# Attention's product with v and the dense projection follow three slots behind a head's scores instead of two

## The chip, the cores and the metric

The kernel runs on one core of one Trainium2 chip. The metric is the time of one execution on the device in microseconds. Besides that there is one profiled execution of the kernel before, whose trace is read below.

## What is computed

Input x is 8 items of 512 rows by 256 columns, in float32. Three blocks follow each other: a feed-forward block, attention, and the feed-forward block once more, each on the layer-normed x and added to x. The change lies in attention alone, which is, cut to what matters:

```python
q  = (ln(x) @ w_q)                       # 16 heads of 128 columns
k, v = split(ln(x) @ w_kv)               # 4 groups of 128 columns each; 4 heads share a group
scores = q @ k.T * 128**-0.5             # 512 x 512 per item and head, causal
probs  = softmax(where(causal, scores, -inf))
ctx    = probs @ v                       # 512 x 128 per item and head
x      = x + concat(ctx) @ w_dense
```

## The kernel before

Attention works in slots, one for each item b and head h: `slot(b, h)`, 8 times 16 of them, and then a few more with no new head. Each engine has its own program and calls its own `slot` in the same order, so that the order of the code is the order of the work on each engine, and semaphores tie the engines together. n is a head's number over all items, from 0 to 127. The 512 query rows are 4 tiles, i = 3 down to 0; tile i sees (i + 1) x 128 keys, since the scores are causal.

Every product with float32 data is made of three matmuls (`product`), of a high part and a low part of each operand. So whatever feeds a product is split first: ScalarE writes the high part, VectorE the low one.

What one head goes through:

1. **Scores** (TensorE, `scores`, slot n): tiles 3, 2, then the projection of the next head's q, then tiles 1, 0. There are three banks for four tiles: tile 0 uses tile 3's bank and waits until tile 3's exponential has been taken (`e_done`).
2. **Maximum and exponential**, same slot: VectorE reduces a tile to its negative maximum (L1316), ScalarE takes the exponential (L1406).
3. **Split of the probabilities**, next slot: ScalarE L1415 and VectorE L1332, four tiles in a row at the head of the slot, to 16-bit floats in `prob`. There is one buffer `prob`: tile i may be written when the transfer of the previous head's tile i has landed (`t_landed`). L1332 reads two operands from SBUF, the exponentials and the high half.
4. **Transposing transfers**: the queue of SyncE (`dma_start_transpose`, L1171), four for each head, from `prob` to `turned`. A transfer waits for its tile (`p_lo`) and until GpSimd has emptied that tile of `turned` for the head before (`t_cast`).
5. **Casts** (GpSimd, `cast_turned`, L1470): `turned` in 16 bits to `pT` in 32, four a head. There is one `pT`, so the casts of head n wait until the product with v of head n - 1 is done:

```python
pool.wait_ge(t_landed[i], 16 * (n + 1))
reach(pool, c_ready, n)
pool.tensor_copy(cast(i), turned[:, 0:i + 1, :, i * P:(i + 1) * P]).then_inc(t_cast, 1)
```

6. **Product with v** (`attend`, at the very start of TensorE's slot n + 2): it waits for all four casts of its head.
7. **Split of ctx** (`split_context`): ScalarE L1421 after its four splits of the probabilities, VectorE L1339 after the maximum of tile 3.
8. **Dense projection** (`dense`, slot n + 2, after scores 1 and 0).

Between these lie other products at fixed places (`projections`): q of the next head in nearly every slot, after scores 2; k of the next group at the end of slots 2, 7, 11 and 15; quarters of v at the end of slots 0 and 3 to 6 and inside slots 0 and 1; the transposes of the next item's normed x in slot 14. The layer norm of the next item lies at the end of VectorE's slots 8 to 12. `add_to_x` (L1347, two instructions on VectorE) adds the dense sums of an item at the end of slot 1 of the next.

Of the kernel before, what the change touches and what calls it, by code (L numbers as in the profile page):

```python
# [955 lines left out]
K_COLS = GROUPS * D  # L956
PT_STEP = 3 * P
PT_COLS = 15 * P
PROB_SCALE = 2.0 ** 15
PROB_AT = (0, P, 3 * P, 6 * P)  # L960
PROB_COLS = 10 * P
# [80 lines left out]
def attention_slots(slot):  # L1042

    def run(eng):
        for b in range(B):
            for h in range(HEADS):
                slot(b, h)
        slot(B, 0)
        slot(B, 1)
    return run  # L1050


# [5 lines left out]
def unit(b, h, lag):  # L1058

    item, head = (b, h - lag) if h >= lag else (b - 1, h - lag + HEADS)  # L1060
    number = item * HEADS + head
    if isinstance(b, int) and not 0 <= number < B * HEADS:
        return None
    return item, head, number


def attention(nc, m, w_q, w_kv, w_dense, out):
    with ExitStack() as ctx:
# [112 lines left out]
        def _(pe):  # L1181
# [60 lines left out]
            def dense(u, half):  # L1242
                b, h, n = u
                if half == 0:
                    pe.wait_ge(c_lo, n + 1)
                if h == 0:

                    reach(pe, x_added, 2 * b - 1 + half)
                for t in (2 * half, 2 * half + 1):
                    mm = product(dn[half][:, (t % 2) * C:(t % 2 + 1) * C], lambda a: cT[:, h % 2, a, t * P:(t + 1) * P],  # L1250
                                 lambda c: wd[:, c, 0, h * C:(h + 1) * C], h == 0 and t % 2 == 0, h == HEADS - 1)
                if h == HEADS - 1:
                    mm.then_inc(d_ready, 1)

            def slot(b, h):
                now, prev2 = unit(b, h, 0), unit(b, h, 2)

                def place(p):
                    what = projections(h).get(p)
                    if what and has_projection(b, h, what):  # L1260
                        project(b + 1 if h >= 14 and what in NEXT_ITEM else b, use_index(b, h, p), what)

                if prev2:
                    attend(prev2)
                if now:
                    scores(now, 3)
                    scores(now, 2)
                place("B")
                if now:
                    scores(now, 1)  # L1270
                    scores(now, 0)
                place("C")
                if prev2:
                    dense(prev2, 0)
                place("D")
                if prev2:
                    dense(prev2, 1)
                place("E")
                place("F")

# [5 lines left out]
        def _(dve):  # L1286
# [60 lines left out]
                    dve.tensor_tensor(x, x, dn[half][:], ALU.add).then_inc(x_added, 1)  # L1347

            def slot(b, h):
                now, prev, prev2 = unit(b, h, 0), unit(b, h, 1), unit(b, h, 2)  # L1350

                def place(p):
                    what = projections(h).get(p)
                    if what and has_projection(b, h, what):
                        split(use_index(b, h, p), what)

                if prev:
                    prob_rsum(prev, 0)
                    for i in reversed(range(QT)):
                        split_probs(prev, i)  # L1360
                if now:
                    score_max(now, 3)
                if prev2:
                    split_context(prev2)
                if now:
                    score_max(now, 2)
                    score_max(now, 1)
                    score_max(now, 0)
                place("B")
                if now:  # L1370
                    prob_rsum(now, 2)
                place("C")
                place("D")
                place("E")
                if not (isinstance(b, int) and b >= B - 1):

                    if 8 <= h < 12:
                        layer_norm(b + 1, h - 8)
                    if 9 <= h < 13:
                        layer_norm_apply(b + 1, h - 9)  # L1380
                place("F")
                if h == 1 and prev2:
                    add_to_x(b - 1)

            for t in range(QT):
# [7 lines left out]
        @block.scalar  # L1393
        def _(act):
            def split(n, what):
                raw, hi, _ = use_halves(n, what)
                act.wait_ge(pj_ready, n + 1)
                act.activation(hi, raw, ACT.Copy, scale=SCALE if what[0] == "q" else 1.0).then_inc(pj_hi, 1)

            def exponential(u, i):  # L1400
                _, h, n = u
                act.wait_ge(s_max, done_of(n, i))

                reach(act, p_lo, done_of(n - 1, i))
                at, width = PROB_AT[i], (i + 1) * P
                act.activation(expo[:, at:at + width], scores_bank(i)[:, 0:width], ACT.Exp, bias=s_bias[:, h % 2, i:i + 1],  # L1406
                               accum_out=p_sum[:, h % 2, i:i + 1]).then_inc(e_done, 1)

            def split_probs(u, i):
                _, h, n = u  # L1410
                act.wait_ge(r_done, 4 * n + 4 - i // 2 * 2)

                reach(act, t_landed[i], 16 * n)
                at, width = PROB_AT[i], (i + 1) * P
                act.activation(prob_half(0, i), expo[:, at:at + width].rearrange("p (j k) -> p j k", k=P), ACT.Copy,  # L1415
                               scale=p_factor[:, h % 2, i:i + 1]).then_inc(p_hi, 1)

            def split_context(u):
                _, h, n = u
                act.wait_ge(c_ready, n + 1)  # L1420
                act.activation(cT[:, h % 2, 0], cx[:], ACT.Copy, scale=1.0 / PROB_SCALE).then_inc(c_hi, 1)  # L1421

            def slot(b, h):
                now, prev, prev2 = unit(b, h, 0), unit(b, h, 1), unit(b, h, 2)

                def place(p):
                    what = projections(h).get(p)
                    if what and has_projection(b, h, what):
                        split(use_index(b, h, p), what)

                if prev:
                    for i in reversed(range(QT)):
                        split_probs(prev, i)
                if prev2:
                    split_context(prev2)
                if now:
                    exponential(now, 3)
                    exponential(now, 2)
                place("B")
                if now:  # L1440
                    exponential(now, 1)
                place("C")
                if now:
                    exponential(now, 0)
                place("D")
                place("E")
                place("F")

            for n, what in enumerate(PROLOGUE):
                split(n, what)  # L1450
            attention_slots(slot)(act)
# [85 lines left out]
```

## Time and profile before

| | |
|---|---|
| median of 3 runs | 2898.04 us (2894.21 to 2900.98) |
| the profiled execution's own time | 2891.25 us |
| its span | 2889.5 us |
| mean granted clock of TensorE in the span | 0.975 |
| first feed-forward block | 0 to about 852 us |
| weights of attention, then its slots | to about 885 us, then 885 to 2051 us |
| second feed-forward block | 2051 us to the end |
| TensorE busy over the span | 2683.8 us (93%) |
| VectorE, ScalarE, GpSimd busy | 2175.4, 947.2, 910.9 us |

Times in the timelines are microseconds from the span's start, so that slots can be laid beside each other. Busy time counts overlapping instructions of an engine once. In brackets behind an instruction stands how long its engine had been idle before it, and who released it.

### The profile page before, as it was taken

The numbers are of one execution on the slowest core, as the hardware profiler recorded it, in microseconds if no ns is written. First come the engines' busy times: TensorE is split into PE (matmuls) and PEld (weight loads), VectorE is DVE, ScalarE is ACT, GpSimd is POOL, SyncE is SP. The second block draws the span as 40 slices with busy tenths as digits, with TensorE's granted clock in tenths as the row PEclk, the third lists the DMA queues.
The fourth block names the chain that finished last, engine by engine and source line by source line (L and its number), as shares of the span: only waits on it lengthen the run. The fifth ranks groups of instructions, "written<-read, shape, count | busy, mean of one in ns | idle before, by whom it ended". The sixth has DMA issues, their size and how long they took to land. (4 is left out here: it accounts for less than half of the span.)

```text
span 2889.5 us, 47699 instructions
## 1 busy us (share of the span) xinstructions
PE 2683.8 (93%) x15460; PEld 2424.8 (84%) x15460; DVE 2175.4 (75%) x5550; ACT 947.2 (33%) x2560; POOL 910.9 (32%) x1944
## 2 busy tenths in 40 slices
PE   6999999999967898989998989898799999999998
PEld 5999999999956787778787877777699999999997
DVE  5888888888866676667776777666678888888887
ACT  3111111111115666656665666666311111011110
POOL 4332333323212333233433333333333333323331
PEclk8999999999988999999999999999799999999999
DMA  6000000000022333333333333333400000000000
GB/s 175 1 1 1 1 1 1 1 1 1 1 72 47 74 74 74 71 74 75 75 74 74 74 74 74 75 72 74 126 19 8 1 8 9 8 1 8 9 8 8
DMA packets 386935, 117.43 MB, mean 41 GB/s; under 512 B 346752, under 2 KB 385664, under 8 KB 386688
## 3 DMA queue, kind: packets, MB, share of 16 engines
q1 hardware_dynamic: 386688, 114.39, 17.8%
q8 instruction: 124, 2.03, 0.3%
q14 instruction: 123, 1.01, 0.1%
HBM read 26.24 MB, written 4.19 MB: 11 GB/s over the span
## 5 line engine op out<-in xcount | busy, mean ns | idle before, releaser
L444 PE MATMUL ffn_ring<-ffn_mix_weights,ffn_yT 128*128 128x384 f32 x6144 | 1250.7, 345 | 16.3 <-DVE ffn_mix_weights L672 8.5
L444 PEld LDWEIGHTS ffn_ring<-ffn_mix_weights,ffn_yT 128*128 128x128 f32 x6144 | 1087.8, 191 | 61.4 <-issue 8.7
L611 DVE SCALAR_TENSOR_TENSOR ffn_mix_sums<-ffn_ring,ffn_w,ffn_mix_sums 128x384 f32<-128x384 f32 x896 | 550.9, 616 | 247.0 <-PE ffn_ring L444 228.0
L1470 POOL CAST attn_probsT<-attn_turned 128x1024 fp32r<-128x1024 f16 (+3 forms) x512 | 372.8, 735 | 726.8 <-DMA attn_turned<-attn_probs 683.8
L495 PE MATMUL ffn_ring<-ffn_out_weights,ffn_avT 128*128 128x512 f32 x1536 | 440.8, 398 | 3.1 <-POOL ffn_avT L903 3.1
L1316 DVE TENSOR_REDUCE attn_score_neg_max<-attn_scores 128x1 f32<-128x512 f32 (+3 forms) x512 | 248.5, 488 | 190.3 <-PE attn_scores L1220 181.7
L1185 PE MATMUL attn_ctx<-attn_probsT,attn_v 128*128 128x256 f32 (+2 forms) x1536 | 290.0, 340 | 97.6 <-POOL attn_probsT L1470 97.3
L1185 PEld LDWEIGHTS attn_ctx<-attn_probsT,attn_v 128*128 128x128 f32 x1536 | 251.8, 197 | 133.9 <-POOL attn_probsT L1470 114.0
L1185 PE MATMUL attn_scores<-attn_kT,attn_qT 128*128 128x256 f32 (+2 forms) x1536 | 328.5, 342 | 11.7 <-ACT attn_exponentials L1406 10.2
L1406 ACT ACTIVATE attn_exponentials<-attn_scores,attn_score_neg_max 128x512 f32<-128x512 f32 (+3 forms) x512 | 268.2, 527 | 168.9 <-DVE attn_score_neg_max L1316 165.8
L495 PEld LDWEIGHTS ffn_ring<-ffn_out_weights,ffn_avT 128*128 128x128 f32 x1536 | 283.0, 189 | 29.1 <-POOL ffn_avT L903 4.6
L1185 PEld LDWEIGHTS attn_scores<-attn_kT,attn_qT 128*128 128x128 f32 x1536 | 248.0, 194 | 31.6 <-ACT attn_exponentials L1406 12.2
L626 DVE SCALAR_TENSOR_TENSOR x<-ffn_ring,ffn_w_out,x 128x256 f32<-128x256 f32 x512 | 247.8, 484 | 17.2 <-PE ffn_ring L495 10.2
L1332 DVE SCALAR_TENSOR_TENSOR attn_probs<-attn_exponentials,attn_prob_factor,attn_probs 128x512 f16<-128x512 f32 (+3 forms) x512 | 253.7, 556 | 8.6 <-ACT attn_probs L1415 8.4
L1415 ACT ACTIVATE attn_probs<-attn_exponentials,attn_prob_factor 128x512 f16<-128x512 f32 (+3 forms) x512 | 249.8, 553 | 28.9 <-DVE attn_prob_factor L1325 25.3
L630 DVE SCALAR_TENSOR_TENSOR ffn_out_odd<-ffn_ring,ffn_w_out,ffn_out_odd 128x256 f32<-128x256 f32 x448 | 212.8, 475 | 0.0
L1185 PE MATMUL attn_projections<-attn_zT,attn_wq 128*128 128x512 f32 x768 | 211.8, 410 | 1.0 <-DVE attn_zT L1311 1.0
L1185 PE MATMUL attn_dense<-attn_wd,attn_ctxT 128*128 128x256 f32 x1536 | 209.4, 284 | 2.8 <-DVE attn_ctxT L1339 2.8
L764 ACT ACTIVATE ffn_yT<-ffn_transposes 128x256 fp32r<-128x256 f32 x64 | 24.6, 384 | 566.0 <-PE ffn_transposes L415 565.9
L1185 PEld LDWEIGHTS attn_dense<-attn_wd,attn_ctxT 128*128 128x128 f32 x1536 | 188.9, 189 | 3.8 <-DVE attn_ctxT L1339 3.2
L1185 PEld LDWEIGHTS attn_projections<-attn_zT,attn_wq 128*128 128x128 f32 x768 | 136.6, 191 | 24.7 <-DVE attn_zT L1311 1.4
L901 POOL CAST ffn_avT<-ffn_av 128x128 fp32r<-128x128 f32 x64 | 18.5, 290 | 430.8 <-DVE ffn_av L665 430.8
(134 smaller groups left out, 2740.4 us busy)
## 6 DMA issues: line engine op xcount, KB each, us to landing
attn_turned<-attn_probs SPq DMA_TRANSPOSE x512, 2.5
ffn_mix_stage<-in_L_ffn_q_proj_dram SPq DMA_DIRECT2D x32, 128.0 KB, 2.6
ffn_mix_stage<-in_L_ffn_k_proj_dram SPq DMA_DIRECT2D x32, 128.0 KB, 2.6
ffn_mix_stage<-in_L_ffn_v_proj_dram SPq DMA_DIRECT2D x32, 128.0 KB, 3.0
ffn_out_stage<-in_L_ffn_o_proj_dram SPq DMA_DIRECT2D x16, 256.0 KB, 3.4
out_dram<-x SPq DMA_DIRECT2D x8, 512.0 KB, 3.0
x<-in_L_attn_x_dram SPq DMA_DIRECT2D x7, 512.0 KB, 8.0
attn_weight_stage<-in_L_attn_w_q_dram SPq DMA_DIRECT2D x4, 512.0 KB, 8.8
```

Of the source, the lines that this page charges most:

```text
L444: last = pe.matmul(bank[:, 0:QKV], yT[:, t % 2, h, k * P:(k + 1) * P], wm[:, e, wh, k], start=(n == 0), stop=(n == 3 * CK - 1))
L495: last = pe.matmul(bank[:], avT[:, t % 2, h], wo[:, g, wh], start=(i == 0), stop=(i == 2))
L611: dve.scalar_tensor_tensor(into, bank[:, 0:QKV], w[:, t, e:e + 1], into, ALU.mult, ALU.add).then_inc(mix_done, 1)
L626: dve.scalar_tensor_tensor(x, bank[:, 0:C], wt[:, 2 * g:2 * g + 1], x, ALU.mult, ALU.add)
L630: dve.scalar_tensor_tensor(odd[:, t % 2], bank[:, C:2 * C], wt[:, 2 * g + 1:2 * g + 2], odd[:, t % 2], ALU.mult, ALU.add).then_inc(out_don ...
L764: act.activation(yT[:, t % 2, 0], tr[:, 0:C], ACT.Copy).then_inc(yT_hi, 1)
L1185: mm = pe.matmul(out_ap, stationary(a), moving(c), start=first and n == 0, stop=last and n == 2, skip_group_check=True)
L1316: dve.tensor_reduce(s_bias[:, h % 2, i:i + 1], scores_bank(i)[:, 0:(i + 1) * P], AX.X, ALU.max, negate=True).then_inc(s_max, 1)
L1332: dve.scalar_tensor_tensor(prob_half(1, i), expo[:, at:at + width].rearrange("p (j k) -> p j k", k=P), p_factor[:, h % 2, i:i + 1], prob_h ...
L1406: act.activation(expo[:, at:at + width], scores_bank(i)[:, 0:width], ACT.Exp, bias=s_bias[:, h % 2, i:i + 1], accum_out=p_sum[:, h % 2, i: ...
L1415: act.activation(prob_half(0, i), expo[:, at:at + width].rearrange("p (j k) -> p j k", k=P), ACT.Copy, scale=p_factor[:, h % 2, i:i + 1]). ...
L1470: pool.tensor_copy(cast(i), turned[:, 0:i + 1, :, i * P:(i + 1) * P]).then_inc(t_cast, 1)
```

## The change

The distance between a head's scores and its product with v and dense projection becomes a constant, `LAST_LAG = 3`, in the programs of TensorE, VectorE and ScalarE. `unit(b, h, lag)` gives the head that lies `lag` slots back. `attend`, `dense` and `split_context` now work on the head of three slots ago. The split of the probabilities stays one slot behind, and the programs of SyncE and GpSimd are as before. There is one more slot after the last head, and `add_to_x` moves from slot 1 to slot 2. No buffer is added.

```diff
+LAST_LAG = 3
@@ attention_slots
-        slot(B, 0)
-        slot(B, 1)
+        for h in range(LAST_LAG):
+            slot(B, h)
@@ TensorE
-                now, prev2 = unit(b, h, 0), unit(b, h, 2)
+                now, last = unit(b, h, 0), unit(b, h, LAST_LAG)
...
-                if prev2:
-                    attend(prev2)
+                if last:
+                    attend(last)
...
-                if prev2:
-                    dense(prev2, 0)
+                if last:
+                    dense(last, 0)
                 place("D")
-                if prev2:
-                    dense(prev2, 1)
+                if last:
+                    dense(last, 1)
@@ VectorE
-                now, prev, prev2 = unit(b, h, 0), unit(b, h, 1), unit(b, h, 2)
+                now, prev, last = unit(b, h, 0), unit(b, h, 1), unit(b, h, LAST_LAG)
...
-                if prev2:
-                    split_context(prev2)
+                if last:
+                    split_context(last)
...
-                if h == 1 and prev2:
+                if h == LAST_LAG - 1 and last:
                     add_to_x(b - 1)
@@ ScalarE
-                now, prev, prev2 = unit(b, h, 0), unit(b, h, 1), unit(b, h, 2)
+                now, prev, last = unit(b, h, 0), unit(b, h, 1), unit(b, h, LAST_LAG)
...
-                if prev2:
-                    split_context(prev2)
+                if last:
+                    split_context(last)
```

## Rows read from the trace of the kernel before

**Rows 1.** Windows, attention: length, busy (instructions) of PE, PEld, DVE, ACT, POOL; clock; DMA; GB/s

```profile
885.00:2052.00 1167.00, 1053.73 (x6508) 896.50 (x6508) 801.05 (x2017) 725.41 (x1914) 399.87 (x568) 0.98 0.36 73
```

**Rows 2.** Waits, 870 to 2075 us: engine, line, releaser; us in total, times, longest

```profile
PE attn_ctx L1185 <- POOL attn_probsT L1470: 97.3, 67, 4.0
```

**Rows 3.** One line (L1171), SyncE's transfers: ns min/median/max; issue to landing

```profile
L1171 SPq DMA_TRANSPOSE attn_turned<-attn_probs x512: 1183/1232/2698, 893.7 to 2040.7; - x171
...
DMA to landing us min/median/max: 2.3/2.5/4.8
```

**Rows 4.** Timeline, slot after a k projection: start, us, engine, line, what

```profile
1248.77 2.10 PE L1185 MATMUL attn_ctx<-attn_probsT,attn_v 128*128 128x512 f32 x12
...
1250.47 1.93 DVE L1332 SCALAR_TENSOR_TENSOR attn_probs<-attn_exponentials,attn_prob_factor,attn_probs 128x512 f16<-128x512 f32 x4
...
1252.32 0.68 DVE L1316 TENSOR_REDUCE attn_score_neg_max<-attn_scores 128x1 f32<-128x512 f32 x1
...
1253.98 0.60 PE L1185 MATMUL attn_scores<-attn_kT,attn_qT 128*128 128x256 f32 x3
...
1257.06 1.27 DVE L1332 SCALAR_TENSOR_TENSOR attn_probs<-attn_exponentials,attn_prob_factor,attn_probs 128x512 f16<-128x512 f32 x2
```

**Rows 5.** Timeline, slot that starts at 1312.83 us (item's last head)

```profile
1312.83 2.18 PE L1185 MATMUL attn_ctx<-attn_probsT,attn_v 128*128 128x512 f32 x12
...
1315.99 0.69 DVE L1316 TENSOR_REDUCE attn_score_neg_max<-attn_scores 128x1 f32<-128x512 f32 x1
...
1317.54 0.63 PE L1185 MATMUL attn_scores<-attn_kT,attn_qT 128*128 128x256 f32 x3 [0.66 <-ACT attn_exponentials L1406]
```

**Rows 6.** Timeline of PE and of POOL: a product with v and the cast it releases

```profile
1259.40 3.89 PE L1185 MATMUL attn_ctx<-attn_probsT,attn_v 128*128 128x512 f32 x12 [3.31 <-POOL attn_probsT L1470]
...
1263.42 1.04 POOL L1470 CAST attn_probsT<-attn_turned 128x1024 fp32r<-128x1024 f16 x1 [3.21 <-PE attn_ctx L1185]
```

**Rows 7.** Groups by shape (L1470): all casts of the two widest tiles

```profile
L1470 POOL CAST attn_probsT<-attn_turned 128x1024 fp32r<-128x1024 f16 x128 | 133.4, 1042 | 575.8 <-DMA attn_turned<-attn_probs 542.9 <-PE attn_ctx L1185 33.0
...
L1470 POOL CAST attn_probsT<-attn_turned 128x768 fp32r<-128x768 f16 x128 | 106.2, 829 | 15.3 <-DMA attn_turned<-attn_probs 7.0
```

**Rows 8.** Timeline: VectorE's four splits with one narrow cast, then with two casts

```profile
2012.27 2.08 DVE L1332 SCALAR_TENSOR_TENSOR attn_probs<-attn_exponentials,attn_prob_factor,attn_probs 128x512 f16<-128x512 f32 x4
2012.80 0.48 POOL L1470 CAST attn_probsT<-attn_turned 128x256 fp32r<-128x256 f16 x1 [0.69 <-DMA attn_turned<-attn_probs]
...
1929.40 2.43 DVE L1332 SCALAR_TENSOR_TENSOR attn_probs<-attn_exponentials,attn_prob_factor,attn_probs 128x512 f16<-128x512 f32 x4
1929.73 1.57 POOL L1470 CAST attn_probsT<-attn_turned 128x512 fp32r<-128x512 f16 x2 [2.16 <-DMA attn_turned<-attn_probs]
```

**Rows 9.** Timeline, slot after a quarter of v at the end of the slot before

```profile
1184.24 2.10 PE L1185 MATMUL attn_ctx<-attn_probsT,attn_v 128*128 128x512 f32 x12
...
1187.33 0.68 DVE L1316 TENSOR_REDUCE attn_score_neg_max<-attn_scores 128x1 f32<-128x512 f32 x1
```

**Rows 10.** Timeline, a slot with layer norm, to the splits of the next

```profile
1272.27 0.68 DVE L1316 TENSOR_REDUCE attn_score_neg_max<-attn_scores 128x1 f32<-128x512 f32 x1
...
1278.03 1.93 DVE L1332 SCALAR_TENSOR_TENSOR attn_probs<-attn_exponentials,attn_prob_factor,attn_probs 128x512 f16<-128x512 f32 x4
```

**Rows 11.** Group of L1347 (`add_to_x`)

```profile
L1347 DVE TENSOR_TENSOR x<-x,attn_dense 128x512 f32<-128x512 f32 x16 | 10.3, 680 | 1.1 <-PE attn_dense L1185 1.1
```

**Rows 12.** Timeline of PE: the first two products with v

```profile
900.97 3.89 PE L1185 MATMUL attn_ctx<-attn_probsT,attn_v 128*128 128x512 f32 x12 [3.18 <-POOL attn_probsT L1470]
...
912.30 1.04 PE L1185 MATMUL attn_ctx<-attn_probsT,attn_v 128*128 128x512 f32 x4
```

**Rows 13.** Timeline: the last two products with v, the last dense projection

```profile
2036.19 2.20 PE L1185 MATMUL attn_ctx<-attn_probsT,attn_v 128*128 128x512 f32 x12 [0.59 <-POOL attn_probsT L1470]
...
2043.49 3.75 PE L1185 MATMUL attn_ctx<-attn_probsT,attn_v 128*128 128x512 f32 x12 [2.04 <-POOL attn_probsT L1470]
...
2048.65 1.64 PE L1185 MATMUL attn_dense<-attn_wd,attn_ctxT 128*128 128x256 f32 x12 [1.41 <-DVE attn_ctxT L1339]
```

## The prediction, as it was made

> **What bounds the kernel now.** I read the page's busy shares first, then the windows by stage, then the waits of the attention stage, and last the timeline of single slots. Of the 1167 us of attention TensorE is busy 1053.7 us, VectorE 801 us, GpSimd 400 us [rows 1]: TensorE sets the pace, and its idle time is 113.3 us. The table of waits names almost all of it: 67 times the matmuls of `attend` stand waiting for the casts of GpSimd, 97.3 us in all [rows 2]. The casts in turn wait for transposing transfers. A transfer takes SyncE's queue 1.23 us and lands 2.5 us after its issue [rows 3], four in a row, so with the cast behind them the chain from a head's split to its `attend` is longer than many slots are. Where no such wait is met, a slot runs at TensorE's own pace. So what the change aims at is real, and bounded: those 97.3 us, and what TensorE's clock loses around the longest waits.
>
> **What it removes.** With three slots in between, the casts of a head are done a slot before its `attend`. Casts of head n are still tied to `attend` of head n - 1, which now starts slot n + 2; they end in that slot, and `attend` of n starts slot n + 3. The wait goes. Of the 97.3 us, 3.2 lie in the first slot with an `attend` [rows 12] and 0.6 + 2.0 in the last two [rows 13], costed below; the middle is 91.5 us. The lower clock: after its longest waits `attend` takes up to 3.89 us instead of 2.10 [rows 4, 6], the granted clock being at the lower of its two levels, 1.2 instead of 2.4 GHz, for a part of it. The mean of 0.98 in attention [rows 1] is 2% of 1167 us, 23 us of full speed, part of it lost while TensorE waited anyway. I take 10 us, between 0 (new waits take the old ones' place) and 20.
>
> **What it moves, the head.** The first `attend` and dense leave slot 2. Before, slot 2 lasted from 900.97 - 3.18 = 897.8 to 912.3 us, 14.5 us [rows 12]. Without those two, the wait and the low clock I count some 7.4 us of ScalarE and VectorE work from one slot's splits to the next (an estimate from 1257.06 - 1250.47 = 6.6 [rows 4], with k's split added). Gain 7.1 us. **The tail.** A third slot without scores follows. Before, from the first of them (2036.19 - 0.59 = 2035.6) to the last dense projection's end (2048.65 + 1.64 = 2050.3) it takes 14.7 us [rows 13]. Now three rounds: `attend` 2.2, 1.41 for the split of ctx, dense 1.64 make 5.3 us [rows 13]; the second and third start when the casts that waited for the `attend` before are done, 2.2 + 0.13 + 1.04 + 0.83 + 0.62 + 0.40 = 5.2 us (the durations below). So 16.2 us, 1.5 more.
>
> **What it moves, the casts.** This is the part that decides. Now the casts come at the pace of landing transfers. The transfer can't go out before the first split is made, so with 2.5 us to landing [rows 3] the first cast comes more than 1.70 + 2.5 = 4.2 us into the slot, when VectorE's splits are over (1.70 + 1.93) [rows 4]; only the narrow last ones reach the next slot's splits. After the change all four have their data long before, and start one behind the other when `attend` ends. `attend` takes 2.10 us [rows 4], and GpSimd starts 0.13 us behind its end (1263.42 - 1259.40 - 3.89) [rows 6], so 2.23 us into every slot, for 2.9 us: the casts take 1.04 and 0.83 us [rows 7], and by their slope of 0.21 us for 256 elements the two narrow ones 0.62 and 0.40. At that time VectorE is in its four splits of the probabilities: in the slot after a k projection they start 1.70 us into the slot and last 1.93 [rows 4]. The trace shows what a meeting costs: with one cast of 0.40 us between them the four splits take 2.08 instead of 1.93 us, with casts of 0.62 and 0.40 us they take 2.43, and the casts themselves stretch too (0.48, and 1.57 for the two) [rows 8]. So the two engines take turns. A cast of 0.40 costs VectorE 0.15, one of 0.62 costs 0.35, which is the cast's length less 0.26; by the same rule the casts of 1.04 and 0.83 us, which hardly meet a split now, cost 0.78 and 0.57.
>
> The Trainium skill, SBUF — State Buffer, section "Who interferes with whom", gives the mechanism a name: a VectorE instruction with two SBUF inputs contends with a GpSimd instruction that reads SBUF, and by it the second to issue is blocked until the first finishes. By that rule each meeting would cost the cast's whole length; here 1.02 us of casts cost 0.50 us, about half of it [rows 8]. What the sum would be by the full length is a rival below.
>
> How late VectorE may be: TensorE needs the bank of tile 3 for tile 0's scores 5.21 us into a slot (1253.98 - 1248.77) [rows 4]. That bank is free 1.55 us after VectorE's maximum of tile 3 starts (1317.54 - 1315.99) [rows 5]. So the maximum may start 3.66 us in; what it starts later, TensorE waits.
>
> - After k (slots 0, 3, 8, 12): the maximum starts 3.55 us in now [rows 4]. The first split runs on, three follow behind casts of 1.04, 0.83 and 0.62 us: 0.78 + 0.57 + 0.35 = 1.70, less some overlap at the first, 1.56. It starts at 5.1, a wait of 1.45 us.
> - After full layer norm (slots 10, 11): from the maximum to the next splits 5.76 us [rows 10] against 4.74 with a lighter norm [rows 4]; I take 5.3, between them, as VectorE there also meets late casts that will be gone. TensorE's next slot could begin 2.11 us after tile 0's scores (1259.40 - 3.31 - 1253.98) [rows 4, 6], so 1.55 + 2.11 = 3.66 us after the maximum if it waits. So the splits start 1.6 us in, as after k: 1.4 us.
> - After a quarter of v, and in slots 9 and 13 (seven slots: 1, 4 to 7, 9, 13): the maximum at 3.09 [rows 9], splits from about 1.2 us in, two behind casts: 0.78 + 0.57 = 1.35, less overlap 1.25. At 4.3, a wait of 0.65.
> - Slot 15 has no q projection ahead of scores 1 and 0 and waits already, 0.66 us [rows 5], so VectorE's delay counts whole: 1.3. Slots 2 and 14, with nothing extra before them: the last split alone meets a cast; 0.2 together, a guess between 0 and 1.
> - `add_to_x` is 2 x 0.68 us [rows 11], and stood ahead of slot 2's splits, under a wait. It moves ahead of slot 3's, which are late after k: 0.8 more there.
>
> An item: 4 x 1.45 + 2 x 1.4 + 7 x 0.65 + 1.3 + 0.2 + 0.8 = 15.5 us. Eight items make 124, less 8 for the first slots of the first item and for the last item's missing layer norm: 116 us. Bounds: nothing, if VectorE's splits get ahead of the casts; 186 by the full length (16 x 0.26 x 3 to 2 casts more).
>
> **The sum.** 91.5 + 10 + 7.1 - 1.5 = 107 us gained, 116 us lost: +9 on the profiled execution's 2891.25 us, 2900. That execution lies 6.8 us below the median of the runs shown, so against them 2907 us. The waits change their name and place, from `attend` to scores of tile 0.
>
> **Rivals.**
> 1. *The splits win part of the turns.* After v the third split is issued some 0.1 us to either side of the cast. If it comes first only one split is delayed, and the maximum starts at 3.7, no wait. Then only the late slots pay: 15.5 less 4.55, 1.3 and 0.2 is 9.5 an item, 48 us less: 2859 us. For it: the margin is tenths. Against it: after a quarter of v VectorE's maximum is already at 3.09 us and starts the moment the splits are over [rows 9], so they start 1.2 us in, a little behind.
> 2. *No toll worth the name*, because casts of 1.04 us yield where narrow ones did not. The whole gain stays: 2907 - 116 + 8 = 2799 us (`add_to_x` makes slot 3 late by itself: 3.55 + 1.3 is 1.2 over 3.66, seven times). This is the case on the other side together with rival 1; it decides as soon as the toll is under some 98 us. For it: no row shows a wide cast meeting a split.
> 3. *The full length.* Each meeting costs 0.26 us more: some 3 x 6 + 2 x 8 = 34 meetings an item, 8.8 us, 70 in all: 2977 us. Rows 8 speak against it.
> 4. *The transfers' loop.* Transfers now wait for casts that wait for `attend`: first cast done at 2.23 + 1.04 = 3.3, the last of four issued 3 x 1.23 later and landed 2.5 after that [rows 3], 9.5 us after the slot's start. ScalarE wants to overwrite the last tile some 2 us into the next slot, the shortest being 1259.40 - 3.31 - 1248.77 = 7.32 us long [rows 4, 6]: 9.3. Mostly even. Stragglers (longest 4.8 us to landing, 2.7 on the queue [rows 3]) used to have a us or more of slack there and lose it: a tenth of the slots (13) by 1.5 us is 20 us: 2927.
>
> **How the numbers follow.** Forecast case 0.42 (2885 to 2935); rival 1 0.25 (2830 to 2885), rival 2 0.12, rival 3 0.09, rival 4 0.12. A measurement of this kernel tells about 0.2%, 6 us, from no change. Faster: 0.25 + 0.12 + 0.05 of the forecast case = 0.42; same (2892 to 2904) 0.12; slower 0.46. The range 2825 to 2950 leaves out rival 2 and most of rival 3; since both signs hold much of the chance, the forecast case's own range stands above.
>
> **What would show it.** Right: no wait of `attend` for casts; casts released by `attend`, not by transfers; all four 2.2 to 5.5 us into the slot; VectorE's four splits at 3.2 to 3.6 us instead of 1.93 where they start late; TensorE's scores of tile 0 waiting for exponentials, some 110 us in place of 10; fewer long `attend`s. Wrong: splits still at 1.93 us would mean rival 2; ScalarE's splits waiting for transfers, rival 4; casts stretched and splits not, rival 1. What would break the sum most easily is the toll per meeting, which I take from narrow casts and apply to wide ones, 34 times an item.

## The result, and the profile after

The changed kernel takes 2917.62 us (median of 5 runs, 2911.47 to 2920.84) against 2898.04: a ratio of 1.0064, with a 95% interval of 1.0047 to 1.0081. It is some 19 us slower, or 0.6%, which is small but clear of the spread of the runs. The profiled execution took 2917.62 us, span 2915.8.

The busy times on the page of the changed kernel:

```profile
PE 2684.2 (92%) x15460; PEld 2429.6 (83%) x15460; DVE 2315.7 (79%) x5550; ACT 931.4 (32%) x2560; POOL 938.4 (32%) x1944
```

The windows of its attention stage (columns as in [rows 1]), and its waits there (columns as in [rows 2]):

```profile
885.00:2080.00 1195.00, 1058.22 (x6508) 904.17 (x6508) 940.60 (x2013) 709.59 (x1914) 427.25 (x568) 0.98 0.33 71
```

```profile
POOL attn_probsT L1471 <- PE attn_ctx L1186: 747.6, 127, 9.2
...
PE attn_scores L1186 <- ACT attn_exponentials L1407: 128.3, 113, 2.6
...
ACT attn_probs L1416 <- DMA attn_turned<-attn_probs: 10.3, 15, 1.4
```

The wait of [rows 2], 97.3 us of `attend` for casts, is gone. In its place TensorE waits 113 times for an exponential, 128.3 us in all, and 112 of these waits stand ahead of tile 0's scores. In the kernel before there were 15 of them (same window as [rows 2]):

```profile
PE attn_scores L1185 <- ACT attn_exponentials L1406: 10.2, 15, 1.2
```

VectorE grew from 801 to 940.6 us with the same instructions [rows 1]. The groups of the two pages say where, before and then after (names, count, then busy us and mean ns, then idle time ahead of them):

```profile
L1332 DVE SCALAR_TENSOR_TENSOR attn_probs<-attn_exponentials,attn_prob_factor,attn_probs 128x512 f16<-128x512 f32 (+3 forms) x512 | 253.7, 556 | 8.6 <-ACT attn_probs L1415 8.4
```

```profile
L1333 DVE SCALAR_TENSOR_TENSOR attn_probs<-attn_exponentials,attn_prob_factor,attn_probs 128x512 f16<-128x512 f32 (+3 forms) x512 | 407.4, 854 | 14.4 <-ACT attn_probs L1416 14.2
```

Those are the splits of the probabilities: the same 512 instructions, 556 ns each before and 854 ns now. One slot shows how they got there. This is the timeline of the slot after a k projection, the same head as in [rows 4] (start, length in us, engine, line, what):

```profile
1250.42 2.10 PE L1186 MATMUL attn_ctx<-attn_probsT,attn_v 128*128 128x512 f32 x12
...
1252.12 3.63 DVE L1333 SCALAR_TENSOR_TENSOR attn_probs<-attn_exponentials,attn_prob_factor,attn_probs 128x512 f16<-128x512 f32 x4
...
1252.65 3.36 POOL L1471 CAST attn_probsT<-attn_turned 128x1024 fp32r<-128x1024 f16 x4 [6.24 <-PE attn_ctx L1186]
...
1255.68 0.68 DVE L1317 TENSOR_REDUCE attn_score_neg_max<-attn_scores 128x1 f32<-128x512 f32 x1
...
1257.22 0.62 PE L1186 MATMUL attn_scores<-attn_kT,attn_qT 128*128 128x256 f32 x3 [1.40 <-ACT attn_exponentials L1407]
```

The casts now have their data (they waited for `attend`, not for a transfer), begin 2.23 us into the slot, in the middle of the splits, and the splits take 3.63 us instead of 1.93. The maximum starts 5.26 us into the slot instead of 3.55. TensorE waits 1.40 us for the bank.

### The profile page after: what moved, and what is told of

Its sections match the earlier page's. It is cut to its first block and busy times, and to the rows that moved or that the text cites. A ratio compares the mean times of both kernels' runs of the same rounds, so it can differ in the third digit from the quotient of the medians.

```text
span 2915.8 us, 47699 instructions
## 1 busy us (share of the span) xinstructions
PE 2684.2 (92%) x15460; PEld 2429.6 (83%) x15460; DVE 2315.7 (79%) x5550; ACT 931.4 (32%) x2560; POOL 938.4 (32%) x1944
## 3 DMA queue, kind: packets, MB, share of 16 engines
q14 instruction: 123, 1.01, 0.1%
## 5 line engine op out<-in xcount | busy, mean ns | idle before, releaser
L1471 POOL CAST attn_probsT<-attn_turned 128x1024 fp32r<-128x1024 f16 (+3 forms) x512 | 404.9, 829 | 769.9 <-PE attn_ctx L1186 747.6
L1186 PE MATMUL attn_scores<-attn_kT,attn_qT 128*128 128x256 f32 (+2 forms) x1536 | 338.3, 341 | 129.8 <-ACT attn_exponentials L1407 128.3
L1333 DVE SCALAR_TENSOR_TENSOR attn_probs<-attn_exponentials,attn_prob_factor,attn_probs 128x512 f16<-128x512 f32 (+3 forms) x512 | 407.4, 854 | 14.4 <-ACT attn_probs L1416 14.2
L1317 DVE TENSOR_REDUCE attn_score_neg_max<-attn_scores 128x1 f32<-128x512 f32 (+3 forms) x512 | 237.2, 481 | 47.0 <-PE attn_scores L1221 46.0
L1186 PE MATMUL attn_ctx<-attn_probsT,attn_v 128*128 128x256 f32 (+2 forms) x1536 | 271.2, 326 | 0.0
L1186 PEld LDWEIGHTS attn_ctx<-attn_probsT,attn_v 128*128 128x128 f32 x1536 | 243.6, 190 | 19.8
L1186 PE MATMUL attn_dense<-attn_wd,attn_ctxT 128*128 128x256 f32 x1536 | 219.7, 293 | 4.8 <-DVE attn_ctxT L1340 4.8
L1186 PE MATMUL attn_projections<-attn_zT,attn_wq 128*128 128x512 f32 x768 | 217.8, 420 | 1.0 <-DVE attn_zT L1312 1.0
L1186 PEld LDWEIGHTS attn_dense<-attn_wd,attn_ctxT 128*128 128x128 f32 x1536 | 199.6, 198 | 6.6 <-DVE attn_ctxT L1340 5.4
```

The lines of the kernel that those rows point to most:

```text
L1186: mm = pe.matmul(out_ap, stationary(a), moving(c), start=first and n == 0, stop=last and n == 2, skip_group_check=True)
L1317: dve.tensor_reduce(s_bias[:, h % 2, i:i + 1], scores_bank(i)[:, 0:(i + 1) * P], AX.X, ALU.max, negate=True).then_inc(s_max, 1)
L1333: dve.scalar_tensor_tensor(prob_half(1, i), expo[:, at:at + width].rearrange("p (j k) -> p j k", k=P), p_factor[:, h % 2, i:i + 1], prob_h ...
```

## The experiments

Each ratio is to the kernel before, timed on the same chip: its median was 2898.0 us beside e1 to e4, 2895.57 beside e5 to e8, 2890.55 beside e9 to e11. Two of the eleven, e3 and e4, have one run each.

**e1: casts only behind the next head's four splits.** In the changed kernel, on GpSimd, ahead of a head's first cast:

```
+ if i == QT - 1 and n + 1 < B * HEADS:
+     pool.wait_ge(p_lo, done_of(n + 1, 0))
```

> The changed kernel, and GpSimd's four casts of a head wait for VectorE's four splits of the next head's probabilities (one wait ahead of the first cast). Theory (casts and splits take turns at SBUF): the splits are back at 1.93 us (now 2.4 to 3.6), TensorE's waits for exponentials fall from 128 us to 10 to 25 us, and nothing takes their place, since the casts still end a slot ahead of the product with v: 2917 less some 110, plus 20 for transfers that start 1 us later and stragglers among them: 2826 us, 2800 to 2860. Rival (the loop of casts, transfers and the overwriting of the probabilities is what limits at three slots): the later casts make it worse, ScalarE's waits for transfers grow from 10 us to over 100, and the time is 2900 or more. Rival (the third slot's order costs by itself, whatever the casts do): no change, 2917.

Measured: 2893.58 us, ratio 0.9987 (0.9976 to 0.9999). Splits and casts no longer meet, but the time hardly moved. Its waits, and its group of splits:

```profile
ACT attn_probs L1416 <- DMA attn_turned<-attn_probs: 190.6, 243, 3.1
DVE attn_probs L1333 <- ACT attn_probs L1416: 151.2, 207, 3.0
...
PE attn_scores L1186 <- ACT attn_exponentials L1407: 105.5, 96, 2.9
```

```profile
L1333 DVE SCALAR_TENSOR_TENSOR attn_probs<-attn_exponentials,attn_prob_factor,attn_probs 128x512 f16<-128x512 f32 (+3 forms) x512 | 264.9, 549 | 153.5 <-ACT attn_probs L1416 151.2
```

The splits are back at 549 ns each, so the meetings were what made them long. But ScalarE now waits 190.6 us to overwrite `prob` until transfers have read it. That is the loop of the prediction's rival 4: a later cast empties `turned` later, the transfer goes out later, the split of the next head waits. In the slot whose `attend` starts at 1185.51 us ScalarE's second split stands 1.81 us for a transfer. The theory had put this loop at 20 us and missed by 68; of the expectation's first rival, the loop itself, the wait came as said (over 100 us) and the time nearly (2900 or more). So the run shows half of the point: the meetings lengthen the splits. What they cost in time it can't show, since another wait took their place.

**e2: the same wait, one split earlier** (`done_of(n + 1, 1)`: the last split may meet the first cast).

> As the run before, but the casts wait only for three of the four splits, so that the first cast (1.04 us) may meet the narrowest split. Theory: the last split is held up by some 0.7 us where it comes behind the cast, which makes the maximum of tile 3 start at about 3.6 us in early slots (no wait) and 4.3 in late ones (0.6 us of wait in six of sixteen slots): 20 to 30 us slower than the run before. If meetings of a wide cast and a split cost next to nothing, equal to it, or faster by the 0.4 us that the transfers start earlier.

Measured: 2856.0 us, 0.9854 (0.9835 to 0.9872), 37.6 us faster than e1. The waits:

```profile
ACT attn_probs L1416 <- DMA attn_turned<-attn_probs: 115.0, 139, 2.6
...
PE attn_scores L1186 <- ACT attn_exponentials L1407: 80.8, 82, 2.8
```

The theory missed again, and in its sign: with casts one narrow split earlier (0.34 us, the least of the splits' durations in e1) ScalarE waits 75.6 us less for transfers, which is worth far more than the 14 us that the splits grew (279.1 us). So a little time of the casts costs much where they sit in a closed loop, and e1's time was set by that loop.

**e3 and e4: the kernel before, with four more instructions of GpSimd on each head.** They stand where the changed kernel has its casts, behind `attend`, and write the same `pT`, which the real casts then write again. In e3 they are copies that read the weights of v; in e4 they only write zeros. (`extra` counts them, and the real casts wait for it.)

```
+ if i == QT - 1:
+     reach(pool, c_ready, n)
+     for k in reversed(range(QT)):
+         pool.tensor_copy(cast(k), <weights of v, same size>).then_inc(extra, 1)   # e3
+         pool.memset(as_f32(cast(k)), 0.0).then_inc(extra, 1)                      # e4
+     pool.wait_ge(extra, QT * (n + 1))
```

> The kernel before (two slots), and GpSimd makes four more copies a head, of the casts' sizes, from the weights of v (SBUF) into the place of the casts, as soon as the product with v has read it; the real casts follow and overwrite them. They start 2.2 us into the slot, where the changed kernel has its casts. Theory: VectorE's splits stretch to 2.4 to 3.6 us and the scores of tile 0 wait for exponentials, as in the changed kernel, with the waits of the product with v kept besides: 2970 to 3060 us. Rival (not the meetings but the change of order costs): splits at 1.93, within 30 us of the kernel before.

> As the run before, but the four extra GpSimd operations only write (memset of the same places), read nothing. If splits and casts fight over a read path alone, as the Trainium skill's page SBUF — State Buffer, section Who interferes with whom, has it for two SBUF inputs against a GpSimd instruction that reads: splits at 1.93 us, and the time within 30 us of the kernel before (GpSimd's busy time alone may delay a cast). If any GpSimd work on SBUF holds up the splits: as with the copies.

Measured: e3 2934.2 us, e4 2893.46 us, one run each. The groups of the splits, e3 and then e4:

```profile
L1332 DVE SCALAR_TENSOR_TENSOR attn_probs<-attn_exponentials,attn_prob_factor,attn_probs 128x512 f16<-128x512 f32 (+3 forms) x512 | 361.2, 766 | 6.7 <-ACT attn_probs L1415 6.7
```

```profile
L1332 DVE SCALAR_TENSOR_TENSOR attn_probs<-attn_exponentials,attn_prob_factor,attn_probs 128x512 f16<-128x512 f32 (+3 forms) x512 | 253.5, 556 | 9.5 <-ACT attn_probs L1415 9.4
```

With copies the splits grow by 108 us and TensorE waits 71.8 us for exponentials; with writes at the same place they stay at 253.5 us, to 0.2 us what they were. So it is GpSimd's reading of SBUF that holds VectorE up, not its being busy, and with no change of lag at all. The Trainium skill, SBUF — State Buffer, section "Who interferes with whom", says the same: an instruction of VectorE with two SBUF inputs contends with one of GpSimd that reads SBUF, not with one that only writes it. The two traces agree, 361.2 against 253.5 us. e3 fell short of its expected 2970. The expectation had kept the waits of `attend` for casts besides, and they fell, from 97.3 to 64.4 us: part of the new wait replaced the old one. The splits grew less than in the changed kernel, too (361.2 against 407.4 us); why, no run was made for.

**e5: two buffers `turned` in the changed kernel.** It opens the loop: a transfer waits for the casts of two heads back. To make room only the tiles below the diagonal are kept, and `pT` is laid out in 13 tiles.

```
- turned = sb("turned", [P, QT, HL, SEQ], F16)
+ turned = sb("turned", [P, 2, HL * PROB_COLS], F16)
+ pT4 = sb("probsT", [P, HL, 13, P], F32R)
...
- reach(sp, t_cast, done_of(n - 1, i))
+ reach(sp, t_cast, done_of(n - 2, i))
+ sp.dma_start_transpose(landed(n, i), prob_halves(i)).then_inc(t_landed[i], 16)
```

> The changed kernel with two buffers for the transposed probabilities (turned) in place of one, so that transfers of a head no longer wait for casts of the head before; casts and splits still meet. The toll of the meetings alone is left. Theory (the meetings are what costs in the changed kernel, the transfers' loop hardly binds yet): ScalarE's 10 us of waits for transfers go, TensorE's waits for exponentials stay near 128 us, 2900 to 2917 us. Rival (the loop costs as much already): below 2880 us.

Measured: 2914.18 us, 1.0073 (1.0047 to 1.01). ScalarE's wait for transfers falls from 10.3 to 2.8 us, TensorE's stays:

```profile
PE attn_scores L1186 <- ACT attn_exponentials L1407: 130.3, 113, 2.6
...
ACT attn_probs L1416 <- DMA attn_turned<-attn_probs: 2.8, 2, 2.1
```

So in the changed kernel itself the loop costs next to nothing, and rival 4 is not why it is slower.

**e6: e5 with e1's wait.** Now neither meeting nor loop.

> Two buffers for the transposed probabilities, and the casts wait for the four splits of the next head. Neither meetings nor the loop of casts, transfers and overwriting. Theory (the run with the wait alone gained only 24 us because the later casts pushed the transfers and ScalarE's overwriting of the probabilities behind them, 191 us of waits there): ScalarE's waits for transfers fall below 20 us, splits at 1.93 us, waits for exponentials 10 to 25 us, 2800 to 2835 us. Rival (something else holds TensorE at three slots): 2860 us or more.

Measured: 2770.74 us, 0.9575 (0.955 to 0.96), 29 us better than the best end expected, which had no term for TensorE's busy time. Windows and waits of its attention, and one slot:

```profile
885.00:1931.00 1046.00, 1018.85 (x6508) 878.53 (x6508) 778.56 (x2014) 713.16 (x1914) 368.83 (x568) 1.00 0.39 82
```

```profile
PE attn_scores L1186 <- ACT attn_exponentials L1407: 20.3, 25, 2.4
...
ACT attn_probs L1416 <- DMA attn_turned<-attn_probs: 9.8, 15, 2.3
```

```profile
1189.75 2.10 PE L1186 MATMUL attn_ctx<-attn_probsT,attn_v 128*128 128x512 f32 x12
...
1190.97 1.94 DVE L1333 SCALAR_TENSOR_TENSOR attn_probs<-attn_exponentials,attn_prob_factor,attn_probs 128x512 f16<-128x512 f32 x4
...
1192.83 0.68 DVE L1317 TENSOR_REDUCE attn_score_neg_max<-attn_scores 128x1 f32<-128x512 f32 x1
...
1193.07 2.72 POOL L1473 CAST attn_probsT<-attn_turned 128x1024 fp32r<-128x1024 f16 x4 [5.12 <-DVE attn_probs L1333]
...
1197.58 2.10 PE L1186 MATMUL attn_ctx<-attn_probsT,attn_v 128*128 128x512 f32 x12
```

The maxima, which have one input and that in PSUM, run beside the casts at their old length (0.68 us), and the casts take 2.72 us together. That is less than their summed lengths, since the spans of successive instructions overlap a little in the profile (four of the mean length of 721 ns are 2.88 us; four splits of 546 ns are 2.18 us and take 1.94). Of the 149 us that the stage is shorter than in the changed kernel (1195 to 1046), waits for exponentials are 108.0 and TensorE's busy time 39.4 us (1058.22 to 1018.85).

**e7: `add_to_x` earlier.** In the changed kernel its place in slot 2 of VectorE goes ahead of the layer norm's (`place("E")`).

```
+ if h == LAST_LAG - 1 and last:
+     add_to_x(b - 1)
  place("E")
```

> The changed kernel, and add_to_x stands in slot 2 ahead of the split of k instead of behind it, where VectorE waits some 2 us for ScalarE's half of k. Theory: slot 3's splits start 1.3 us earlier, and TensorE's wait in slot 3 is some 0.8 to 1.3 us shorter, seven times: 6 to 9 us less than the changed kernel. Rival (slot 3's lateness is absorbed): no difference.

Measured: 2906.62 us, 1.0047 (1.0029 to 1.0065); waits for exponentials 123.3 us, five less. The interval of its ratio and the changed kernel's overlap, so its own gain is not settled by this run.

**e8, e9, e10: all of it, with casts behind three, four or two splits** (two `turned`, `add_to_x` earlier, and a wait for `done_of(n + 1, 1)`, `0` or `2`).

> Two buffers for the transposed probabilities, casts wait for three of the next head's four splits, add_to_x ahead of the split of k. Beside the second run of this call it has add_to_x earlier (6 us less) and the first cast may meet the narrowest split (up to 0.7 us in six of sixteen slots, up to 40 us more, if theory's price holds when there is no loop to relieve; nothing, if the maximum has slack): 2800 to 2850 us.

> Two buffers for the transposed probabilities, casts wait for all four splits, add_to_x ahead of the split of k: the one edit that lay between the second and the fourth run of the last call besides the shorter wait. Theory (there is no meeting and no loop left, so moving the start of the casts by 0.4 us changes nothing, and add_to_x alone made the difference of 9.5 us): 2761 us, within 4 us of the kernel with the shorter wait. Rival (the shorter wait helps): 2766 to 2771.

> As the kernel with two buffers, the wait for three splits and add_to_x earlier (2761 us), but the casts wait for two splits only, so the first cast comes where the third split ends or the fourth begins, and is sure to hold up at least one. Theory: a meeting of the 1.04 us cast with the fourth split delays the maximum of tile 3 by up to 0.7 us, which late slots (6 of 16) hand to TensorE: 10 to 35 us slower, 2770 to 2800. Rival (one meeting has slack everywhere): 2757 to 2765.

Measured: e8 2761.29 us, 0.9545 (0.952 to 0.957); e9 2758.42, 0.9542 (0.9527 to 0.9556); e10 2813.22, 0.9724 (0.971 to 0.9739). Behind three splits or four is one and the same; with two splits left to meet casts it costs 55 us by the medians of e10 and e9. The waits of e9 and then of e10, then the splits and the window of e10's attention:

```profile
PE attn_scores L1186 <- ACT attn_exponentials L1407: 13.4, 17, 2.1
```

```profile
PE attn_scores L1186 <- ACT attn_exponentials L1407: 40.6, 55, 1.5
```

```profile
L1333 DVE SCALAR_TENSOR_TENSOR attn_probs<-attn_exponentials,attn_prob_factor,attn_probs 128x512 f16<-128x512 f32 (+3 forms) x512 | 341.3, 728 | 10.0 <-ACT attn_probs L1416 9.9
```

```profile
885.00:1978.00 1093.00, 1040.34 (x6508) 887.46 (x6508) 867.45 (x2014) 707.09 (x1914) 388.81 (x568) 1.00 0.36 78
```

Loop and `add_to_x` are alike in the three, so this is a measure of the meetings alone: 92.5 us of longer splits (341.3 less e9's 248.8) cost 55 us. Of these 27 are waits for exponentials, and 21 are busy time of TensorE (1040.34 against e9's 1018.89 us), though its granted clock is 1.00 in both. e9 is the fastest kernel of this study, 4.6% under the kernel before. Against e6 `add_to_x` is worth 9.5 us by e8's run beside it, and as much by the ratios of e9 and e6, whose intervals overlap a little.

**e11: two `turned` in the kernel before** (two slots, no wait added).

> The kernel before (two slots) with two buffers for the transposed probabilities alone. Theory (at two slots a transfer never waits for a cast; the wait of the product with v is the chain of splits, four issues on the queue, landing and cast): no change, 2888 to 2905 us, waits of the product with v 90 to 105 us. Rival (the second buffer is worth something by itself, and the good kernels owe it that): 2880 or less.

Measured: 2889.87 us, 1.0001 (0.9988 to 1.0014), `attend` waiting 94.4 us for casts. The second buffer by itself is worth nothing, so the 4.25% of e6 need the third slot. That the wait for the splits would do as little at two slots no run shows. It is likely, since the splits of the kernel before took 253.7 us and those of e9, with nothing beside them, 248.8: there were 5 us of meetings to avoid.

## Why the prediction was right, and where it was not

The forecast was 2907 us, its own case 2885 to 2935; 2917.62 lies in it, on the side forecast. By its steps:

- **The wait removed.** It said that `attend` would wait for no cast; no such row is left. 97.3 us are gone, as said.
- **The toll, 116 us.** TensorE's waits for exponentials grew from 10.2 to 128.3 us, by 118. This is the step on which the most hung, and it was right in nearly all its parts too. These are the scores of tile 0 in the slots that follow the one above, and ahead of them slot 3, then slot 1:

```profile
1265.17 0.63 PE L1186 MATMUL attn_scores<-attn_kT,attn_qT 128*128 128x256 f32 x3 [0.59 <-ACT attn_exponentials L1407]
...
1273.87 0.61 PE L1186 MATMUL attn_scores<-attn_kT,attn_qT 128*128 128x256 f32 x3 [1.33 <-ACT attn_exponentials L1407]
...
1282.59 0.62 PE L1186 MATMUL attn_scores<-attn_kT,attn_qT 128*128 128x256 f32 x3 [1.36 <-ACT attn_exponentials L1407]
...
1293.80 0.63 PE L1186 MATMUL attn_scores<-attn_kT,attn_qT 128*128 128x256 f32 x3 [2.46 <-ACT attn_exponentials L1407]
```

```profile
1212.38 0.62 PE L1186 MATMUL attn_scores<-attn_kT,attn_qT 128*128 128x256 f32 x3 [2.33 <-ACT attn_exponentials L1407]
```

```profile
1188.70 3.29 DVE L1333 SCALAR_TENSOR_TENSOR attn_probs<-attn_exponentials,attn_prob_factor,attn_probs 128x512 f16<-128x512 f32 x4
1189.71 3.10 POOL L1471 CAST attn_probsT<-attn_turned 128x1024 fp32r<-128x1024 f16 x4 [7.78 <-PE attn_ctx L1186]
...
1193.46 0.61 PE L1186 MATMUL attn_scores<-attn_kT,attn_qT 128*128 128x256 f32 x3 [0.58 <-ACT attn_exponentials L1407]
```

These rows and the other slots of the same item (its slots 0 to 15; the sums of the trace's waits):

| slot | after | expected wait, us | measured, us |
|---|---|---|---|
| 0, 8 | k | 1.45 | 1.39, 1.40 |
| 9 | nothing wide | 0.65 | 0.59 |
| 10, 11 | full layer norm | 1.4 | 1.33, 1.36 |
| 12 | k (and layer norm) | 1.45 | 2.46 |
| 13, 14 | nothing wide | 0.65, about 0.1 | 0.56, 0.59 |
| 15 | no q ahead of scores 1 and 0 | 0.66 + 1.3 | 1.98 |
| 1, 4 to 7 | quarter of v | 0.65 | 0.58 to 0.61 |
| 2 | nothing | about 0.1 | 0 |
| 3 | k, `add_to_x` | 2.25 | 2.33 |

  Two entries are off by more than a tenth of a us. Slot 12 comes after k and behind a slot with layer norm, and the prediction counted it as any slot after k; it had already waited 0.69 us in the kernel before, so its wait grew by 1.77. Slot 14 waited in this item where hardly anything was said; over the eight items slots 13 and 14 each waited in four and not in the other four. The item's waits add up to 17.0 us and were 1.35 before: 15.6 more, where 15.5 was said. That the sum is so near is partly luck, as slots 12 and 14 and the small shortfalls of most others cancel.
- **The rule for a meeting.** It took from narrow casts that a cast costs the splits its length less 0.26 us, and used it for wide ones. Three casts (1.04, 0.83, 0.62, together 2.49 us) should cost 1.70, before the 0.14 that the prediction took off for the first; in slot 8 the splits grew from 1.93 to 3.63, by 1.70. Rival 2 (wide casts yield) and rival 3 (the whole length, 2.49) fall here, and rival 1 with slot 1: the splits after v took 3.29 us and TensorE waited, so they did not slip ahead of the casts. Rival 3 took the toll to be 186 us, and two thirds of it were measured.

  The Trainium skill, SBUF — State Buffer, section "Who interferes with whom", has the second to issue blocked until the first finishes, from which rival 3 came. By the profile's lengths the splits of slot 8 do not agree with it (1.70 us for 2.49 us of casts), and for a cost the measurement decides. Whether a cast holds VectorE up during its whole profiled length no run shows: the spans of successive casts overlap by themselves (e6), so part of the 0.26 us may lie in how they are recorded.
- **Head and tail.** The first `attend` starts at 904.80 us, the last tail lasts from 2064.23 to 2080.0, 15.8 us, where 16.2 was said:

```profile
904.80 2.10 PE L1186 MATMUL attn_ctx<-attn_probsT,attn_v 128*128 128x512 f32 x12
...
2064.23 2.08 PE L1186 MATMUL attn_ctx<-attn_probsT,attn_v 128*128 128x512 f32 x12
...
2078.36 1.65 PE L1186 MATMUL attn_dense<-attn_wd,attn_ctxT 128*128 128x256 f32 x12 [1.41 <-DVE attn_ctxT L1340]
```

  The head gained 7.5 us where 7.1 was said: slot 3 starts at 904.80 us, and in the kernel before it started at 912.30 [rows 12]. The tail took 14.7 us before [rows 13].
- **The clock, 10 us gained, and TensorE's busy time.** In the two profiles the granted clock of attention is 0.98 before and after [rows 1], and both traces' clock records have the lower level for 44.4 us of it: nothing gained. But single profiles differ here. Take as lost time 1 less the granted clock, times the length. Attention loses 22, 29 and 31 us in the profiles of the kernel before, e4 and e11, which have two slots and nearly the same waits, and 22, 15 and 17 us in those of the changed kernel, e5 and e7, which have three slots and its waits: 9 us less on average. Over the timed runs the mean loss of a whole execution is 74 to 79 us in the kernel before (its three sets of runs beside the experiments) and 62 in the changed kernel, 11 to 17 less. So the 10 us were about right. What the sum had no term for shows in TensorE's busy time in attention, which went up from 1053.73 to 1058.22 us. Its groups, first of the kernel before (a window from 885 to 2080 us):

```profile
L1185 PE MATMUL attn_scores<-attn_kT,attn_qT 128*128 128x256 f32 (+2 forms) x1536 | 328.5, 342 | 11.7 <-ACT attn_exponentials L1406 10.2 <-DVE attn_kT L1311 1.5
L1185 PE MATMUL attn_ctx<-attn_probsT,attn_v 128*128 128x256 f32 (+2 forms) x1536 | 290.0, 340 | 97.6 <-POOL attn_probsT L1470 97.3
L1185 PE MATMUL attn_dense<-attn_wd,attn_ctxT 128*128 128x256 f32 x1536 | 209.4, 284 | 2.8 <-DVE attn_ctxT L1339 2.8
L1185 PE MATMUL attn_projections<-attn_zT,attn_wq 128*128 128x512 f32 x762 | 208.9, 408 | 0.0
```

  The same of the changed kernel:

```profile
L1186 PE MATMUL attn_scores<-attn_kT,attn_qT 128*128 128x256 f32 (+2 forms) x1536 | 338.3, 341 | 129.8 <-ACT attn_exponentials L1407 128.3 <-DVE attn_kT L1312 1.5
L1186 PE MATMUL attn_ctx<-attn_probsT,attn_v 128*128 128x256 f32 (+2 forms) x1536 | 271.2, 326 | 0.0
L1186 PE MATMUL attn_dense<-attn_wd,attn_ctxT 128*128 128x256 f32 x1536 | 219.7, 293 | 4.8 <-DVE attn_ctxT L1340 4.8
L1186 PE MATMUL attn_projections<-attn_zT,attn_wq 128*128 128x512 f32 x762 | 214.9, 418 | 0.0
```

  And of e6, with 25 waits left:

```profile
L1186 PE MATMUL attn_scores<-attn_kT,attn_qT 128*128 128x256 f32 (+2 forms) x1536 | 324.6, 338 | 22.7 <-ACT attn_exponentials L1407 20.3 <-DVE attn_kT L1312 1.5 <-DVE attn_v L1312 0.9
L1186 PE MATMUL attn_ctx<-attn_probsT,attn_v 128*128 128x256 f32 (+2 forms) x1536 | 269.0, 324 | 0.4 <-POOL attn_probsT L1473 0.4
L1186 PE MATMUL attn_dense<-attn_wd,attn_ctxT 128*128 128x256 f32 x1536 | 209.5, 284 | 4.4 <-DVE attn_ctxT L1340 4.4
L1186 PE MATMUL attn_projections<-attn_zT,attn_wq 128*128 128x512 f32 x762 | 208.9, 408 | 0.0
```

  `attend` did get 18.8 us back (290.0 to 271.2), as said. The new waits stand elsewhere, and the work there slowed in this profile: dense by 10.3 us, the projections of q by 6.0. The prediction put what the clock takes behind the new waits only into the lower bound of its term. **The term that was missing** is that of the scores: 9.8 us more busy time (328.5 to 338.3) with the same count and no longer mean (342 and 341 ns). It is no chance of one profile: e4 and e11 have 328.8 and 329.2 us, e5 has 337.9. The same work covers more time when its matmuls overlap each other less, and the waits stand in the middle of it. With those gone too (e6) the scores are at 324.6 us, dense and q at 284 and 408 ns again, and the stage has no time at the lower clock.
- **The sum.** Said: 107 gained, 116 lost, +9; the medians differ by 19.6, and the profiled executions by 2917.62 - 2891.25 = 26.4 us. The toll was 2 us more. Not in the sum were the 9.8 us of the scores and two small waits, 4.6 us together: of dense for the split of ctx (2.8 to 4.8 us) and of the transposes of normed x for the split of q (0.5 to 3.1). Head and tail went 0.8 us better. That makes +25. The clock gave back 11 to 17 us instead of 10 over the timed runs, which leaves 18 to 23, and 7.5 instead of 10 in the profiled pair (73.1 to 65.6 us lost in the whole execution), which leaves 27. The sign was less sure than the parts: +9 is the difference of two terms above 100, and with 20 us for the clock, the upper end of its own range, it would have been -1. That it came out slower is owed in part to terms that the prediction did not have.
- **Rival 4, the loop,** costs the changed kernel no more than 10.3 us of ScalarE's waits, and taking them away (e5) gained nothing beyond what the measurement can tell. It was right as a mechanism: when the casts start later still, it becomes the bound (e1, 190.6 us).

What the third slot is worth when its price is not paid e6 shows: 2770.74 us, 4.25% under the kernel before, and 143 us under e5, which differs from it by the wait alone. Against the profile of the changed kernel it has 108.0 us fewer waits for exponentials and 39.4 us less busy time. Not all of the 39.4 us is clock. The profile of the changed kernel loses 22.2 us of attention to the clock and e6 none; the groups place 18 of these (10.2 in dense, 6.0 in q, 2.2 in `attend`). Another 13.7 are in the busy time of the scores (338.3 to 324.6 us), whose mean hardly moves (341 to 338 ns). e10 says what those are not: its scores take 336.7 us at the same mean of 338 ns, with no time at the lower clock. So a wait costs TensorE busy time also where the clock stays up. That the waits hold the clock down is read from the traces; no run varied the waits alone, and e10 kept its clock with 55 of them.

## What to carry to other kernels

When a dependency is loosened, ask at what time the freed work will now run and beside what: here casts that had been paced by transfers moved into the middle of another engine's two-input instructions and brought 118 us of new waits. Before a wait is traded for another of the same total, count what each side costs besides: the clock gave back only some 10 us while 113 waits of up to 2.6 us stood in for 67 of up to 4.0, and the scores around the new waits took 10 us more busy time. Look at more than one profile before a few us are put down to the clock. A constraint that keeps two engines apart is worth adding only when the ring of buffers around it has slack: the same wait was worth 24 us with one `turned` buffer and 143 with two.

## What the runs showed of the hardware

- VectorE's two-input splits and GpSimd's casts from SBUF take turns, and VectorE pays about the cast's profiled length less 0.26 us for each meeting: 0.15 us for a cast of 0.40, 0.35 for 0.62, 1.70 for three of 2.49 together. The casts stretch as well (3.36 us for the four instead of 2.72). VectorE's maxima, whose one input lies in PSUM, kept their 0.68 us beside casts. GpSimd's writes of the same size cost the splits nothing (e4, 556 ns as before).
- With 113 waits of 0.6 to 2.6 us in attention the granted clock was 0.98 and TensorE's busy time 1058 us for 6508 instructions; with 25 left (e6) it was 1.00 and 1019 us. With 55 waits of at most 1.5 us (e10) the clock was 1.00 too, and the busy time still 1040 us.
- Profiles of kernels with the same waits differed in what the clock took from attention by 9 us (22, 29 and 31 us; 22, 15 and 17 us).
- Casts that start one narrow split (0.34 us) earlier were worth 37.6 us (e2 against e1) where the chain of cast, transfer and overwriting closes on itself.
